# Feed-forward's second phase in sixteen half groups, with ScalarE scaling two parts of six and VectorE adding the rows

## The reference, cut to what matters

```python
def _act_fake_quant(x, clip_factor):
    scale = jax.nn.sigmoid(clip_factor) * jnp.max(jnp.abs(x)) / QMAX      # QMAX = 127, one number for the whole tensor
    return jnp.clip(_ste_round(x / scale), -QMAX - 1.0, QMAX) * scale
...
xq = _act_fake_quant(x, clip_x[0])
gate = jnp.einsum('bsh,ih->bsi', xq, _weight_fake_quant(w_gate))          # i = 704
up = jnp.einsum('bsh,ih->bsi', xq, _weight_fake_quant(w_up))
h = _act_fake_quant(jax.nn.silu(gate) * up, clip_down[0])
return jnp.einsum('bsi,hi->bsh', h, _weight_fake_quant(w_down))           # back to 256 columns
...
x = x + jnp.tanh(g_ffn[1]) * _L1_ffn_ref(_layernorm(x, axis=-1), ...)
```

## Time and profile before

| | us |
|---|---|
| median of 3 runs | 2242.48 (2239.87 to 2250.66) |
| the profiled execution | 2242.07 |
| its span, first to last instruction | 2240.00 |
| outside the span | 2.07 |
| second phase: from the first `scaled` at 2188.3 to VectorE's last add at 2237.0 | 48.7 |
| last output DMA landing, after that | 3.0 |

### The profile page before, as it was taken

One profiled execution on the slowest core, in us unless ns is written; L12 is line 12 of the kernel. 1 busy time (PEld: TensorE's weight loads), 2 busy tenths in 40 slices (PEclk: granted clock), 3 DMA queues, 4 the chain that ended last, 5 costly groups with the idle time before them and its releaser, 6 DMA issues.

```text
span 2240.0 us, 39247 instructions
## 1 busy us (share of the span) xinstructions
PE 2029.5 (91%) x14922; PEld 1248.5 (56%) x14922; DVE 1682.1 (75%) x2822; ACT 1221.4 (55%) x2885; POOL 661.8 (30%) x520
## 2 busy tenths in 40 slices
PE   7797889888977899999989999999999988899896
PEld 3454555555545444444456666666666656676643
DVE  5888686776879889977067777777778867676697
ACT  2455876858855666555523333333333367677585
POOL 0305877868767542000000000000000013243353
PEclk6898999999987999999999999999999999999997
DMA  4232000000000466454586666766766670000002
GB/s 120 70 107 61 1 2 1 2 1 3 21 20 1 164 228 240 200 216 175 210 237 197 203 190 200 205 189 195 205 190 204 192 212 16 1 1 2 1 1 75
DMA packets 134331, 255.34 MB, mean 114 GB/s; under 512 B 17868, under 2 KB 62785, under 8 KB 134017
## 3 DMA queue, kind: packets, MB, share of 16 engines
q1 hardware_dynamic: 113616, 185.05, 27.5%
q10 hardware_dynamic: 20529, 67.79, 7.7%
HBM read 169.28 MB, written 82.44 MB: 112 GB/s over the span
## 4 chain that ended last, share of the span: by engine, by line
PE 59%; DVE 21%; ACT 11%; POOL 4%; issue 3%; DMA 1%; SPq 1%; ACTq 0%; DVEq 0%; POOLq 0%
PE ps L519 56%; DVE arena L1042 8%; DVE arena L1051 6%; ACT arena L2006 5%; DVE arena L1045 3%; PE ps L527 3%; ACT arena L1756 3%; DVE arena L1048 2%; POOL arena L2111 2%; POOL arena L2072 1%; ACT arena L2014 1%; DVE arena L1058 1%; SPq L2205 1%; POOL arena L2124 1%; DMA arena<-share_scratch 1%
## 5 line engine op out<-in xcount | busy, mean ns | idle before, releaser
L519 PE MATMUL ps<-arena 128*128 128x512 f16 (+13 forms) x13708 | 1907.4, 297 | 135.1 <-DVE arena L1051 26.5
L519 PEld LDWEIGHTS ps<-arena 128*128 128x128 f16 (+7 forms) x13708 | 1109.9, 102 | 849.3 <-issue 115.6
L1042 DVE TENSOR_TENSOR arena<-arena 128x512 f32<-128x512 f32 (+6 forms) x992 | 715.1, 753 | 145.2 <-ACT arena L1964 92.4
L1756 ACT ACTIVATE arena<-ps,arena 128x512 f32<-128x512 f32 (+3 forms) x512 | 342.3, 686 | 178.0 <-PE ps L519 161.8
L1042 DVE TENSOR_TENSOR arena<-ps,arena 128x512 f16<-128x512 f32 (+11 forms) x440 | 238.8, 568 | 240.4 <-ACT arena L1760 87.2
L2072 POOL TENSOR_TENSOR arena<-arena 128x4 f32<-128x4 f32 (+5 forms) x51 | 85.2, 1672 | 1084.4 <-DVE arena L1045 1083.9
L1964 ACT CAST arena<-arena 128x512 f16<-128x512 f32 x256 | 158.2, 618 | 436.7 <-DVE arena L1042 432.2
L2111 POOL TENSOR_TENSOR arena<-arena 128x512 f16<-128x512 f32 (+1 forms) x288 | 350.8, 1240 | 65.0 <-ACT arena L1756 63.5
L1756 ACT ACTIVATE arena<-ps 128x512 f16<-128x512 f32 (+1 forms) x512 | 275.2, 611 | 89.2 <-PE ps L519 85.1
L1051 DVE TENSOR_REDUCE arena<-ps 128x1 f32<-128x1024 f32 (+5 forms) x246 | 224.5, 919 | 45.7 <-PE ps L519 42.9
L527 PE MATMUL ps<-arena 128*128 128x128 f32 (+4 forms) x1214 | 192.1, 286 | 70.7 <-DVE arena L1042 26.8
(11 more groups left out here) (81 smaller groups left out, 451.7 us busy)
## 6 DMA issues: line engine op xcount, KB each, us to landing
wide_scratch<-arena ACTq DMA_DIRECT2D x128, 512.0 KB, 2.6
arena<-share_scratch SPq DMA_DIRECT2D x512, 128.0 KB, 3.7
arena<-wide_scratch SPq DMA_DIRECT2D x128, 512.0 KB, 4.8
mq_scratch<-arena SPq DMA_DIRECT2D x16, 308.0 KB
vw_scratch<-arena SPq DMA_DIRECT2D x32, 154.0 KB
arena<-mq_scratch SPq DMA_DIRECT2D x16, 308.0 KB, 5.6
arena<-vw_scratch SPq DMA_DIRECT2D x8, 576.0 KB, 6.4
arena<-in_x SPq DMA_DIRECT2D x4, 1024.0 KB, 9.8
```

The costliest lines, as they stand in the source:

```text
L519: return e.matmul(o, l, r, start=start, stop=stop, skip_group_check=True)
L1042: return e.tensor_tensor(o, a, b, op)
L1756: return e.activation(o, i, f, bias=bias, scale=scale)
```

## The change

The second phase goes from 8 groups to 16 half groups h of 256 tokens.

- `scaled(h)` on VectorE covers parts 0 to 3 (4 rows of 256), `scaled_rest(h)` on ScalarE parts 4 and 5 (2 rows of 256, all 128 partitions). Relu and `clipped(h)` work on one half of an `HQ` buffer; Relu waits for PE's half h-4.
- PE does 12 matmuls for each half group. Its second diagonal matmul now stands behind the first half group's 12.
- `finish(g)` becomes `dequantised(g)` and `added(g)`, both on VectorE, one in each odd and the other in each even turn, still 128x1024. GpSimd's loop of adds is gone. The last group is finished in halves as before.

```diff
--- before.py
+++ after.py
@@ -1015,21 +1015,24 @@
             if c == 2 and g < 7:
                 whole(g + 1)
         whole_max(1)
-        claim(7)
-        for k in range(2):
+        def diagonal(k):
             W.wait_ge("dgk", k + 1)
             mm(bank(7)[:, 128 * k:128 * k + 128], ones, dg, True, True).then_inc(S["sdm"], 1)
-        for g in range(8):
+
+        claim(7)
+        for h in range(16):
+            g, u = divmod(h, 2)
             b0 = 2 * (g % 3)
-            claim(b0, b0 + 1)
-            W.wait_ge("hq", g + 1)
-            for t in range(4):
+            if h < 2:
+                diagonal(h)
+            if u == 0:
+                claim(b0, b0 + 1)
+            W.wait_ge("hq", h + 1)
+            for t in range(2):
                 for c in range(6):
                     r_ = 128 if c < 5 else 64
-                    m = mm(bank(b0 + t // 2)[:, 256 * (t % 2):256 * (t % 2) + 256], HQ[g % 2][0:r_, c, 128 * t:128 * t + 128],
+                    m = mm(bank(b0 + u)[:, 256 * t:256 * t + 256], HQ[g % 2][0:r_, c, 256 * u + 128 * t:256 * u + 128 * t + 128],
                            WDq[0:r_, c, :], c == 0, c == 5)
-                if g == 7 and t == 1:
-                    m.then_inc(S["dn"], 1)
             m.then_inc(S["dn"], 1)
             empty[b0] = empty[b0 + 1] = [("y2", g + 1)]
 
@@ -1702,49 +1705,67 @@
                     peak(n - 2)
         W.after(a)
         whole_max(1, hm, 10, 3)
-        W.own(tt(s[:, 12:13], s[:, 10:11], gat[:, 7:8], ALU.mult))
-
-
-        def scaled(g):
-            v = H[:, 0:5, 512 * g:512 * g + 512]
+        weighed = W.own(tt(s[:, 12:13], s[:, 10:11], gat[:, 7:8], ALU.mult))
+
+
+        def scaled(h):
+            v = H[:, 0:4, 256 * h:256 * h + 256]
             ts(v, v, s[:, 11:12], MAGIC, ALU.mult, ALU.add).then_inc(S["ha"], 1)
 
-        def clipped(g):
-            W.wait_ge("hlo", g + 1)
-            ts(HQ[g % 2], HQ[g % 2], 255.0, 128.0, ALU.min, ALU.subtract).then_inc(S["hq"], 1)
-
-        scaled(0)
-        W.last()
-        for k in range(2):
+        def clipped(h):
+            v = HQ[h // 2 % 2][:, :, 256 * (h % 2):256 * (h % 2) + 256]
+            W.wait_ge("hlo", h + 1)
+            ts(v, v, 255.0, 128.0, ALU.min, ALU.subtract).then_inc(S["hq"], 1)
+
+        def diagonal(k):
             W.after(W.own(ts(s[:, 14 + k:15 + k], sw[:, 12 + k:13 + k], s[:, 12:13], None, ALU.mult)))
             W.wait_ge("sdm", k)
             ts(dg, ident, s[:, 14 + k:15 + k], None, ALU.mult).then_inc(S["dgk"], 1)
+
+        scaled(0)
         scaled(1)
-        W.wait_ge("sdm", 2)
-        sd = W.own(cp(SD, bank(7)[:, 0:256]))
+        W.after(weighed)
+        diagonal(0)
+
+        def dequantised(g):
+            b0 = 2 * (g % 3)
+            W.wait_ge("dn", 2 * g + 2)
+            W.wait_ge("fo", g - 1)
+            W.after(sd[0])
+            tt(Y2[g % 2], bank(b0, 2).rearrange("p (t n) -> p t n", t=4), rep(SD.unsqueeze(1), [128, 4, 256]),
+               ALU.mult).then_inc(S["y2"], 1)
+
+        def added(g):
+            v = xs[:, 4 * g:4 * g + 4, :]
+            W.wait_ge("y2", g + 1)
+            tt(v, v, Y2[g % 2], ALU.add).then_inc(S["fo"], 1)
 
         def finish(g):
             b0 = 2 * (g % 3)
-            W.wait_ge("dn", g + 1)
             W.wait_ge("fo", g - 1)
-            W.after(sd)
-            if g < 7:
-                tt(Y2[g % 2], bank(b0, 2).rearrange("p (t n) -> p t n", t=4), rep(SD.unsqueeze(1), [128, 4, 256]),
-                   ALU.mult).then_inc(S["y2"], 1)
-                return
+            W.after(sd[0])
             for u in range(2):
-                W.wait_ge("dn", 8 + u)
+                W.wait_ge("dn", 2 * g + 1 + u)
                 y, v = Y2[1][:, 2 * u:2 * u + 2, :], xs[:, 28 + 2 * u:30 + 2 * u, :]
                 W.after(W.own(tt(y, bank(b0 + u).rearrange("p (t n) -> p t n", t=2), rep(SD.unsqueeze(1), [128, 2, 256]),
                                  ALU.mult)))
                 tt(v, v, y, ALU.add).then_inc(S["y2"], 1)
 
-        for g in range(8):
-            clipped(g)
-            if g < 6:
-                scaled(g + 2)
-            if g:
-                finish(g - 1)
+        sd = []
+        for h in range(16):
+            clipped(h)
+            if h < 14:
+                scaled(h + 2)
+            if h == 0:
+                diagonal(1)
+            elif h == 2:
+                W.wait_ge("sdm", 2)
+                sd.append(W.own(cp(SD, bank(7)[:, 0:256])))
+            elif h % 2 and h > 1:
+                dequantised(h // 2 - 1)
+            elif h > 2:
+                added(h // 2 - 2)
+        added(6)
         finish(7)
 
 
@@ -2047,21 +2068,20 @@
             if c == 3 and g < 7:
                 whole(g + 1)
 
-        def scaled_rest(g):
-            v = H[0:64, 5, 512 * g:512 * g + 512]
-            return W.own(fn(v, v, ACT.Identity, bias=mg[0:64], scale=s[0:64, 11:12]))
+        def scaled_rest(h):
+            v = H[:, 4:6, 256 * h:256 * h + 256]
+            return W.own(fn(v, v, ACT.Identity, bias=mg, scale=s[:, 11:12]))
 
         W.wait_ge("const", 15)
         W.wait_ge("wmd", 8)
-        rest = [scaled_rest(0), scaled_rest(1)]
-        for g in range(8):
-            W.wait_ge("ha", g + 1)
-            W.after(rest[g])
-            W.wait_ge("dn", g - 1)
-            fn(HQ[g % 2], H[:, :, 512 * g:512 * g + 512], ACT.Relu, bias=nml).then_inc(S["hlo"], 1)
-            if g < 6:
-                rest.append(scaled_rest(g + 2))
-
+        rest = [scaled_rest(0)]
+        for h in range(16):
+            W.wait_ge("ha", h + 1)
+            W.after(rest[h])
+            W.wait_ge("dn", h - 3)
+            c0 = 256 * (h % 2)
+            fn(HQ[h // 2 % 2][:, :, c0:c0 + 256], H[:, :, 256 * h:256 * h + 256], ACT.Relu, bias=nml).then_inc(S["hlo"], 1)
+            rest += [scaled_rest(n) for n in ((1, 2) if h == 0 else (h + 2,) if h < 14 else ())]
 
 
 
@@ -2191,10 +2211,6 @@
             e.tensor_tensor(H[:, c, 512 * g:512 * g + 512], FSp[i % 2], UPp[i % 2], ALU.mult).then_inc(S["fhp"], 1)
             if c == 1 and g < 6:
                 whole(g + 2)
-        for g in range(7):
-            v = xs[:, 4 * g:4 * g + 4, :]
-            W.wait_ge("y2", g + 1)
-            e.tensor_tensor(v, v, Y2[g % 2], ALU.add).then_inc(S["fo"], 1)
 
 
 
```

## The result

| | before | with the change |
|---|---|---|
| median of 20 runs each, us | 2241.64 (2232.36 to 2253.62) | 2234.73 (2229.31 to 2249.39) |
| second phase in the profile, first `scaled` to VectorE's last add | 48.70 | 41.79 |
| the phase's start in the profiled execution | 2188.31 | 2200.44 |
| the profiled execution, and its span | 2242.07, 2240.00 | 2246.59, 2244.82 |

The ratio is 0.9967, 95% interval 0.9951 to 0.9983. The change made the kernel 6.9 us faster by the medians, 0.33%, and the interval leaves out 1. In the profile the phase is shorter by 6.91 us. That the two agree so closely is chance: by the interval the gain in the whole time lies between 3.8 and 11.0 us. The profiled execution as a whole is nevertheless longer than that of before, since its second phase began 12 us later.

A forecast was written before the change was run, and what follows sets the result against it. VectorE was taken to bound the second phase, above all by `scaled`, stretched by GpSimd's add. Start, 13 paces of 2.30 and the end sum to 42.4 us instead of 48.7: 2242.07 - 6.3 = 2235.8 us, range 2231.5 to 2242.5.

The forecast's parts named there:

- The bound: Steady second phase before: VectorE bounds it at 5.82 us a group, GpSimd's add costing its `scaled` about 2.1 us.
- the pace: Second phase after: 2.30 us per half group, with 2.24 as the bound; 4.6 per group instead of 5.82.
- an earlier start: Start of the second phase: first half at about 3.1 us instead of 6.55, half a group passing ScalarE before the first matmul.
- Rows counted in pairs: VectorE's `scaled`: five rows cost as six, 1.85 us for 5 x 512, which leaves four rows of 256 at 0.72.
- The rival of the short rows: Each VectorE row costs 0.05 us: `scaled` 0.92, half group 2.74, time 2241.7 us; chance 0.10.
- The 0.05 for handing over: VectorE and ScalarE nearly tied, each handing over twice per half group, so pace taken as 2.30, not 2.24.
- the starting point: The profiled execution before, 2242.07 us, from which the gain of 6.3 was subtracted.
- The rival of the slow clock: PE stays at 1.2 GHz, 16 halves of 2.95 us: 3.8 us slower than before, 2245.9 us; chance 0.08.
- the last half would be done in time: End of the phase: PE's last half runs from 37.5 us, needed at 41.0, so done even at half clock.
- three slow halves in the middle: Half groups at half clock: three in a row are absorbed, the fourth costs; PE falls behind about 0.65 us each.
- the signs of a wrong forecast: Forecast fails if `clipped` is 2.7 apart, VectorE waits for PE several turns, or the 2188.3 us before the phase moves.

The follow-up runs named there:

- adds only: Kernel before with one edit: VectorE does the seven adds of the rows, GpSimd none; second phase 45.18 us against 48.70.
- adds back: Changed kernel with GpSimd adding the rows again, half groups and two parts on ScalarE kept; second phase 48.02 us against 41.79.
- ScalarE's share undone: Changed kernel with ScalarE scaling only the last part again and VectorE five parts; second phase 44.39 us against 41.79.
- eight halves: Changed kernel with 20 instead of 12 matmuls in eight half groups in a row (h = 6 to 13); second phase 43.51 us.

## Why the prediction was right, point by point

- **The bound.** VectorE was the bound of the steady part and `scaled` the instruction that set it, stretched by GpSimd's add. Shown from both sides: adds only (1.814 us throughout) and adds back (+2.08 us per pair). But the steady part of before is only three groups long, from 2206.70 to 2224.16. The prediction put the gain down to the pace and an earlier start; by the table above, 3.6 of the 6.9 us are waits of VectorE's that are gone, 3.05 of them from the end of the phase, where TensorE had been at half clock, and the others from its start. Its forecast did not need this split, since it set a new phase against the measured old one.
- **`scaled` at 0.72, `clipped` at 0.55, add at 1.22.** Measured 0.752, 0.561 and 1.224. Rows counted in pairs is shown by five rows at 1.014 and six at 1.017. The Trainium skill ("Vector Engine (DVE) Microarchitecture Reference", section 5.1) says that the first port takes the larger half of an odd count, and these runs agree with it. Five parts are a bad number for VectorE here and four are cheap. The rival of the short rows is out: four rows of 256 cost 0.03 us more than 1024 plain elements, not 0.20. (Its price was added up wrongly by 0.2 us: 2235.8 + 5.7 is 2241.5, not 2241.7.)
- **ScalarE.** Relu 1.569 and rest 0.803, taken as 1.58 and 0.80. The move of a part to ScalarE brought 2.6 us where I had worked out 3, and 0.4 of the 2.6 came by TensorE's clock. ScalarE's own pace of 2.18 us is seen at the start, where the clips are 2.18 apart. It leaves 0.08 us of room in a half group, so more of this kind can't be moved in the steady part. The rule of the Trainium skill ("ScalarE: Activation LUTs", rules for kernel authors) that such work belongs on VectorE did not hold for this stage, where ScalarE had the time: 44.39 us with VectorE doing it, 41.79 without.
- **The pace.** 2.26 us, taken as 2.30, bound 2.24. The 0.05 for handing over was not paid; from `clipped(1)` to `clipped(14)` 29.27 us passed instead of 29.90, which is the 0.6 us by which the phase came out shorter (41.8 instead of 42.4). The gain was 6.91 us in the phase instead of 6.3. The time, 2234.7 instead of 2235.8, has another 0.4 us from the starting point, 2242.07, where the median of before came out at 2241.64. That the forecast time lies within 1.1 us is in part luck, since single executions of either kernel spread over 20 us.
- **The start and TensorE's clock.** The first matmuls began at 3.1 us, as taken. The low clock at the start cost nothing, and it did not fall again in either profile of the change, with rests of 0.35 to 0.53 us. The rival of the slow clock was nearer than its 0.08 suggests: the clock did fall in two neighbouring kernels, adds back and ScalarE's share undone. In the second, three half groups at half clock at the very end cost 0.39 us; the prediction held that the last half would be done in time even at half clock, but it counted one slow half there, not three. The price of a longer spell is shown for a stand-in: eight halves, each 0.38 us above the pace, cost 1.7 us. That three slow halves in the middle are absorbed fits, since 2.8 us of delay at half group 11 cost nothing. TensorE at half clock through the whole phase did not come about, and its price was not measured.
- **What was not foreseen.** That the phase's start would lie 12 us late in the profile was named among the signs of a wrong forecast. It was a sign of scatter: most of the delay arises 2 ms ahead of the change, between 117 and 141 us, in code that the change doesn't touch, and another execution of the same kernel began the phase 8.7 us earlier than the kernel before did in its profile.

## What to carry to other kernels

An engine that is idle isn't free help: ask what its instruction does to the one that is the bound. Here, in a steady group, a 3 us add on idle GpSimd cost VectorE 2.1 us, more than the 1.22 us that VectorE needs to do it itself. Ask also what the bound waits for outside its steady part: over the whole phase of before GpSimd's adds cost VectorE 8.5 us and its own 8.4, and most of the 3.5 us gained by that step are waits that vanished. When a change is small against the scatter of the runs, compare the length of its stage in the profiles; it repeated to 0.01 us where whole executions differed by 20. And look at the waits that the new order leaves at its start: shifting work there brought another 1.4 us.

## What the runs showed of the hardware that was not expected

- Five rows in the one-source VectorE instruction `scaled` cost as much as six: 5 x 256 f32 in 1.014 us, 6 x 256 in 1.017, 4 x 256 in 0.752. 5 x 512 took 1.815 and 4 x 512 1.283; other odd counts were not tried.
- Beside a GpSimd add of 128x1024 f32, VectorE's own add with both sources in SBUF is stretched too: 128x512 took 2.34 us instead of 0.69. The dequantization of 128x512 from PSUM just ahead of it, the greater part of which also lay beside that add, was not: it and the one of 128x1024 before it took 1.81 us together, which is 1.21 + 0.68 less the usual overlap.
- The granted clock of TensorE differed between executions at one and the same place while TensorE was busy in both: 0.50 in one (busy for 11.45 of 12.00 us) and 0.98 in another (12.00 of 12.00), over 112 to 124 us. What decides it was not tried.
- TensorE's clock fell to half in the middle or at the end of the phase in three kernels, after rests of 2.27 us (before), of 1.34 and 0.53 (adds back) and of 0.79 and 0.63 (ScalarE's share undone). It did not fall in others with rests of 0.35 to 0.53, of 0.77 and of 1.30 us. The length of the rests alone doesn't sort them.
